# Attention stage with its loop written out, the split of x moved to the start of a period, both halves of a projection together, and four stack slots for the first four tiles

## The reference, cut to what matters

```
x: (8, 512, 256) float32;  H = 16 heads of DH = 16
qkv = (x @ Wqkv).reshape(b, l, 3, H, DH);  q, k, v = qkv[:, :, 0], qkv[:, :, 1], qkv[:, :, 2]
q = q * cos + rotate_half(q) * sin;        k = k * cos + rotate_half(k) * sin
attn = softmax(einsum('bqhd,bkhd->bhqk', q, k) * DH ** -0.5)
out = einsum('bhqk,bkhd->bqhd', attn, v).reshape(b, l, d) @ Wo
x = layernorm(x + out)
x = layernorm(x + ffn(x))     # a shared expert and the best 2 of 8 experts
```

## Time and profile before

| | |
|---|---|
| median of 3 runs (1282.54 to 1285.19) | 1282.6 us |
| the profiled execution, own time | 1286.31 us |
| its span | 1284.4 us |
| granted TensorE clock, mean | 0.969 |
| TensorE / VectorE / ScalarE / GpSimd busy | 1174.9 / 970.9 / 895.0 / 582.5 us |

### The profile page before, as it was taken

The page is one execution under the profiler, slowest core; times in us unless marked ns, Lnnn a source line. Parts: engine busy times, 40 slices in busy tenths (PEclk is TensorE's granted clock), DMA queues, the critical chain, the costliest instruction groups (busy, mean ns, idle before and its releaser), DMA issues. The chain is left out here.

```text
span 1284.4 us, 27380 instructions
## 1 busy us (share of the span) xinstructions
PE 1174.9 (91%) x8369; PEld 864.1 (67%) x8416; DVE 970.9 (76%) x1868; ACT 895.0 (70%) x1970; POOL 582.5 (45%) x591
## 2 busy tenths in 40 slices
PE   3799898989898999879899969999999999999997
PEld 2333333333333333247899969999999999999897
DVE  4788787888787888738766658777777777777596
ACT  3377777777677777647744447777777777777686
POOL 5332222232223220006557745666666666666763
PEclk8699999999999999989899979999999999999999
DMA  6743525252537363532032256777777777776363
GB/s 151 137 82 58 112 53 97 63 110 61 130 96 159 85 155 88 170 125 85 17 112 92 96 170 220 258 237 235 249 251 252 237 238 234 249 252 207 131 187 114
DMA packets 260558, 194.45 MB, mean 151 GB/s; under 512 B 152256, under 2 KB 243392, under 8 KB 260480
## 3 DMA queue, kind: packets, MB, share of 16 engines
q1 hardware_dynamic: 253664, 174.82, 48.2%
q0 software_dynamic: 6816, 18.75, 4.1%
HBM read 122.06 MB, written 37.52 MB: 124 GB/s over the span
## 5 line engine op out<-in xcount | busy, mean ns | idle before, releaser
L464 ACT ACTIVATE att_prob<-att_psB 128x512 f32<-128x512 f32 x512 | 298.3, 608 | 133.1 <-PE att_psB L363 114.0
L553 DVE TENSOR_REDUCE att_mx<-att_psA 128x1 f32<-128x512 f32 x512 | 327.9, 681 | 77.3 <-PE att_psA L353 67.4
L353 PE MATMUL att_psA<-att_qk 96*128 96x512 bf16 x512 | 197.6, 390 | 17.6 <-DVE att_mx L553 6.9
L1650 ACT ACTIVATE exp_psU<-exp_psU,ew_b 128x256 f32<-128x256 f32 x312 | 126.9, 446 | 103.8 <-PE exp_psU L1607 103.8
L363 PE MATMUL att_psB<-att_qk 128*128 128x512 bf16 x465 | 178.4, 387 | 10.2 <-DMA att_qk<-att_mrow 6.1
L1701 DVE CAST exp_hh<-exp_psU 128x512 fp32r<-128x512 f32 x156 | 107.8, 691 | 102.4 <-ACT exp_psU L1650 102.4
L1590 PE MATMUL exp_psD<-exp_w2h,exp_hh 128*128 128x256 f32 x624 | 175.8, 282 | 0.0
L1605 PE MATMUL exp_psU<-exp_xh,exp_w1h 128*128 128x256 f32 x624 | 173.8, 279 | 1.4 <-DVE exp_xl L1692 1.4
L1606 PE MATMUL exp_psU<-exp_xl,exp_w1h 128*128 128x256 f32 x624 | 173.4, 278 | 0.0
L1607 PE MATMUL exp_psU<-exp_xh,exp_w1l 128*128 128x256 f32 x624 | 173.4, 278 | 0.0
L1591 PE MATMUL exp_psD<-exp_w2l,exp_hh 128*128 128x256 f32 x624 | 172.5, 276 | 0.0
(11 more groups left out here) (211 smaller groups left out, 2854.3 us busy)
## 6 DMA issues: line engine op xcount, KB each, us to landing
ew_w<-ew SPq DMA_DIRECT2D x40, 1024.0 KB, 4.9
exp_w<-ew SPq DMA_DIRECT2D x38, 1024.0 KB, 5.8
slots_x<-pre_acc SPq DMA_DIRECT2D x13, 780.0 KB, 4.4
pre_spare<-slots_x SPq DMA_DIRECT2D x39, 260.0 KB, 4.2
out_g<-rows_y SPq DMA_DIRECT2D x32, 256.0 KB, 3.9
ew_b<-eb SPq DMA_DIRECT2D x39, 128.0 KB
pre_spare<-xT SPq DMA_DIRECT2D x8, 512.0 KB, 3.9
attn_rows<-att_ob SPq DMA_DIRECT2D x8, 512.0 KB, 2.8
```

What stands on the lines that cost most here:

```text
L353: pe.matmul(psA[A_BANK[n % U]][:, :], r[:, 0, qt * P:(qt + 1) * P], r[:, 1, :], start=True, stop=True).then_inc(s_amm, 1)
L464: act.activation(prob[:, n % PR, :], psB[B_BANK[n % U]][:, :], ACT.Exp, scale=SCALE).then_inc(s_exp, 1)
L553: dve.reduce_max(mx[:, g % 2, n % U:n % U + 1], psA[A_BANK[n % U]][:, :], AX_X).then_inc(s_max, 1)
```

## The change

- The hardware loop goes: all periods are written out, and semaphore values are constants.
- `x_hi` moves from step 14 to step 0 of its period; `x_lo` moves on GpSimd from the end of that period to its start.
- A projection of queries and keys is issued whole after step 0, product by product instead of half by half.
- Steps: `turn_out` 5 to 6, `norm_out` (5, 6) to (6, 7), `rope` (1, 1, 2) to (1, 2, 2), `copy_max` 9 to 11, `piece_1` 7 to 6, `repeat_1` (8, 9) to (7, 8), `piece_2` 10 to 9, `repeat_2` (11, 12) to (10, 11).
- The first operation of the maxima's split is a scalar_tensor_tensor (m x 0 - m) instead of a tensor_scalar (m x -1).
- The first four tiles have four slots: two in `stack` and two in `prob`, which the first exponential then waits for (`s_tr[1]`). Their first halves are turned as they come, the second halves all after the fourth tile's first. ScalarE makes their pieces, VectorE the last piece of the keys. The set-up on GpSimd starts with the slots' padding.
- w is loaded and split in two parts (queries and keys, then V), with x between them. Four of the first projections have banks of their own.
- SyncE clears the slots from period 1 on, behind the transposes, and loads the attention's rows of a sequence some periods after its store.

```diff
-    ASIDE_QK, ASIDE_V = (1, 3), (0, 1)
...
-    PROJECT_QK, ROPE, COPY_OUT, TURN_OUT, NORM_OUT = (0, 1), (1, 1, 2), 3, 5, (5, 6)
-    PROJECT_V, COPY_V, SPLIT_MAX, TURN_MAX, COPY_MAX = 13, 13, 8, 10, 9
-    PIECE_1, SPREAD_1, PIECE_2, SPREAD_2, SPLIT_X = 7, (8, 9), 10, (11, 12), 14
+    PROJECT_QK, ROPE, COPY_OUT, TURN_OUT, NORM_OUT = 0, (1, 2, 2), 3, 6, (6, 7)
+    PROJECT_V, COPY_V, SPLIT_MAX, TURN_MAX, COPY_MAX = 13, 13, 8, 10, 11
+    PIECE_1, SPREAD_1, PIECE_2, SPREAD_2, SPLIT_X = 6, (7, 8), 9, (10, 11), 0
...
+        ASIDE_QK, ASIDE_V = {1: psA[0], 2: psB[0], 3: psB[1]}, {0: psA[1], 1: psA[2]}
...
-            with eng.Fori(0, passes) as it:
-                for p in range(HEAD, HEAD + BODY):
-                    period(p, it)
...
+            for p in range(-QK_LEAD, NG + 1):
+                period(p)
...
+        def stack_of(tile):
+
+            if tile in (2, 3):
+                some = prob[:, PR // 2 * (tile - 2):PR // 2 * (tile - 1), :].rearrange("p n l -> p (n l)").bitcast(BF16)
+                return some.rearrange("p (i h c) -> p i h c", i=2, h=H)
+            return stack[:, tile % 2]
...
+            CLEAR = [p for p in range(NG) for _ in range((1, 1, 2, 0)[p % NT])][1:CHUNKS + 1]
+            ALL_CLEAR = CLEAR[-1] + 2
+            LOAD = NG - 2 * NT
...
                     turn_heads(tile, 0)
-                    if b < 2 or t >= 2:
+                    if b == 0 and t == NT - 1:
+                        for first in range(NT):
+                            turn_heads(first, 1)
+                    elif b == 1 or b > 1 and t >= 2:
                         turn_heads(tile, 1)
-                    elif t == 1:
+                    elif b > 1 and t == 1:
...
+                for c in range(CHUNKS):
+                    if CLEAR[c] == p:
+                        sp.dma_start(slots[c], blank).then_inc(s_zero, 16)
+                if p == ALL_CLEAR:
+                    sp.wait_ge(s_zero, 16 * CHUNKS)
+                for b in range(B - 1):
+                    if p == max(NT * b + 6, ALL_CLEAR + b):
+                        sp.wait_ge(s_ost[b % 2], 16 * (b // 2 + 1))
+                        norm.load_attention(sp, attn_out, b)
...
+                if t == NT - 1 and valid(b + 1 - 2, B - 2):
+                    x_lo(b + 1)
                 if tile >= FILL:
...
-                if t == NT - 1 and valid(tile + 1 - 2 * NT, NT * (B - 2)):
-                    x_lo(b + 1, it)
...
+                for c in range(DC):
+                    pe.matmul(o, xh[:, b % 2, c, rows], wh[:, c, cols], start=(c == 0), stop=False)
+                if tile == 0:
+                    pe.wait_ge(s_wl, 2 if value else 1)
+                for c in range(DC):
+                    pe.matmul(o, xh[:, b % 2, c, rows], wl[:, c, cols], start=False, stop=False)
+                if t == 0 and not value:
+
+                    pe.wait_ge(s_xl, b + 1)
+                for c in range(DC):
+                    m = pe.matmul(o, xl[:, b % 2, c, rows], wh[:, c, cols], start=False, stop=(c == DC - 1))
...
+                if n == 0:
+                    for k in range(2):
+                        act.wait_ge(s_tr[1][k], 32 * NT // 2)
...
-                    link(dve.tensor_scalar(mstk[:, 0, :], m, -1.0, None, ALU.mult))
+                    link(dve.scalar_tensor_tensor(mstk[:, 0, :], m, 0.0, m, ALU.mult, ALU.subtract))
...
+            def piece_3(tile):
+                st = terms(tile)
+                dve.wait_ge(s_p2, tile + 1)
+                dve.tensor_tensor(st[:, H:, 2, :], heads_of(r1)[:, H:], st[:, H:, 4, :], ALU.subtract).then_inc(s_qsp, 1)
...
+            w_lo(0, slice(0, 2 * D))
+            x_lo(0)
+            w_lo(1, slice(2 * D, 3 * D))
+            x_lo(1)
```

More of the change, by code:

```diff
@@ L166, in attention, with wait, groups @@
         s_dve = a.sem("vector_chain")
[L168 to L181, removed]
-            with eng.Fori(0, passes) as it:
-                for p in range(HEAD, HEAD + BODY):
-                    period(p, it)
[L185 to L188, removed]
+        def wait(eng, s, v):
+            if v > 0:
+                eng.wait_ge(s, v)
+        def groups(period):
+            for p in range(-QK_LEAD, NG + 1):
+                period(p)
         def valid(i, n):
@@ L254, in turn_heads @@
                     sp.dma_start_transpose(qk[:, b % 2, i, some, t * P:(t + 1) * P],
[L255 removed]
+                                           stack_of(tile)[:, i, some, :].rearrange("p h c -> p (h c)")).then_inc(s_tr[half][tile % 2], 16)
             def period(p):
@@ L293, in _ @@
         def _(pool):
[L295 to L311, removed]
-                pool.wait_ge(s_init, k + 1)
@@ L313, in x_lo, with put @@
-            def x_lo(b, it):
-                v = b + 1
-                pool.wait_ge(s_xh, v if it is None else v + it * 2)
+            done = [0]
+            def put(ins):
+                ins.then_inc(s_init, 1)
+                done[0] += 1
+                pool.wait_ge(s_init, done[0])
+            for tile in range(NT):
+                put(pool.memset(stack_of(tile)[:, :, :, KR:], 0.0))
+                put(pool.memset(stack_of(tile)[:, 1, :, KR:KR + PIECES], 1.0))
+            assert done[0] == PADDED
@@ new lines, in _ @@
+            put(pool.memset(zero, 0.0))
+            assert done[0] == BLANK
+            for one in (ident, identf):
+                put(pool.memset(one[:, :], 0.0))
+                put(pool.affine_select(out=one[:, :], in_=one[:, :], compare_op=ALU.not_equal, fill=1.0,
+                                       base=0, pattern=[[-1, P]], channel_multiplier=1))
+            put(pool.memset(V[:, :, :, :, DH + 1:], 0.0))
+            put(pool.memset(V[:, :, :, :, DH:DH + 1], 1.0))
+            put(pool.memset(norm.eps[:, 0:1], 1e-5))
@@ L472, in copy_v, with piece_1 @@
                 b, t = tile // NT, tile % NT
-                wait(act, it, s_vmm, tile + 1, 1)
+                wait(act, s_vmm, tile + 1)
                 if t == 0:
-                    wait(act, it, s_pv, NT * HG * (b - 1), NT)
-                bank = psA[1] if it is None and tile in ASIDE_V else psX
+                    wait(act, s_pv, NT * HG * (b - 1))
+                bank = aside(tile, True) or psX
                 act.activation(V[:, b % 2, t, :, 0:DH], bank[:, 0:D].rearrange("p (h d) -> p h d", d=DH), ACT.Copy).then_inc(s_vev, 1)
-            def piece_1(tile, it):
-                wait(act, it, s_rr, tile + 1, 1)
-                for half in range(2):
-                    wait(act, it, s_tr[half][tile % 2], 32 * (tile // 2), 16)
+            def piece_1(tile):
+                wait(act, s_rr, tile + 1)
+                if tile >= FILL:
+                    for half in range(2):
+                        wait(act, s_tr[half][tile % 2], 32 * (tile // 2))
@@ L514, in period @@
+            w_hi(1, slice(2 * D, 3 * D))
+            x_hi(1)
+            def period(p):
                 for u in range(U):
@@ L596, in norm_out, with rope @@
                                       ALU.mult).then_inc(s_onrm, 1)
-            def rope(tile, k, it):
+            def rope(tile, k):
                 b, t = tile // NT, tile % NT
-                x, half = heads_of(psA[0] if it is None and tile in ASIDE_QK else psX), DH // 2
+                x, half = heads_of(aside(tile, False) or psX), DH // 2
                 def table(tb, c0, c1):
```

309 lines of the change are left out of this document (135 added, 174 removed).

## The result

The changed kernel took 1267.21 us (median of 4 runs, 1265.94 to 1268.2), the kernel before 1283.89 beside it: a ratio of 0.9867, 95% interval 0.9846 to 0.9888. The forecast was 1268.0. The profiled execution took 1267.04 us (span 1265.2), 19.3 less than that of before; on the medians it is 16.7.

The account below looks back on a forecast made before the run. TensorE and VectorE were both nearly full in the attention's steady part, so waits between them matter. Terms -16.1 - 4.4 - 6.2 + 5 + 2.5 + 5 + 0 = -14.2, from 1282.6 to 1268.4 us; range 1250 to 1282.

Parts of the forecast that it names:

- x split at step 0: Six periods with an x split lose their extra 3.78 (twice) or 2.13 us (four times): gain 16.1 us.
- No loop: Both turns of the attention's loop go, 2.21 us each, with the waits' register sums: gain 4.4 us.
- Loads spread: Spreading seven 512 KB attention-row loads removes TensorE's 5.22 us wait for the last maxima copy, plus 1.0: gain 6.2 us.
- The order within a period: VectorE's queue delays the maxima copy by 0.80 us against 0.60 slack; 0.20 in each of 25 periods: loss 5 us.
- (a): In VectorE's queue, the maxima copy moves behind two more row maxima, 0.61 us each: +1.22 us.
- (b): The output's multiplication, formerly in an idle stretch of VectorE, now stands on the path to the maxima copy: +0.33 us.
- (c): The first step of the maxima's split no longer waits for GpSimd's subtraction, on VectorE: -0.78 us.
- The last periods: From the 26th period, without projections, two more maxima before the copy cost about 0.6 us in each of four: loss 2.5.
- Instruction blocks: Straight code fetches throughout, so one maxima copy in every fourth of 25 periods lands 0.8 us late: loss 5 us.
- The fill: Before the first maxima copy, sixteen transposes take 22.04 us of issue whatever their order: 0 us, bounds -4 and +3.
- TensorE decides the period: Rival: VectorE is ahead, TensorE's waits are saved, the period is 14.9 us, another -19, so 1249 us; chance 0.22.
- Fetching is hidden: Rival: instruction blocks come while no maxima copy is under way, so their 5 us loss is 0: 1263 us; chance 0.12.

Follow-up runs that it names:

- straight form: The kernel before with only its hardware loop written out as straight code: 1282.86 us, ratio 0.9965 to the kernel before.
- the old form of the split: The changed kernel with the first operation of the maxima's split back as m x -1 with one input: ratio 0.9844 to the kernel before.
- the fill in turn: The changed kernel with both halves of the first four tiles turned as each tile comes: ratio 0.9841 to the kernel before.

## Why the prediction was right, and where its sizes were off

The forecast came out 0.8 us from the median, and its mechanism is the one that the runs show: the gains of the split, the loop and the loads, less a copy of maxima that became the last to arrive. That it is as near as 0.8 us is luck: the forecast counted from 1282.6, three runs of the kernel before; from the 1283.89 measured beside the changed kernel it would be 2.5 us too high, and in the profiled executions 5.0. Its terms, in its own order:

- *x split at step 0 (gain 16.1).* Right in the periods: none is longer any more. What the term hid is that its two sizes are two causes. TensorE's wait for GpSimd makes 17.40; where the granted clock also falls, the mean to 0.91 between the levels of 2.4 and 1.2 GHz, it is 19.05, another 1.65 (so it is in all twelve such periods of the kernel before and its straight form). The prediction took both sizes as they stood. In the changed order the same late split cost 1.62, not 2.13 to 3.78, so of 16.1 us some 6 belong to the order of before.
- *No loop (gain 4.4).* 4.5 us (2.7 to 6.3), measured alone. The prediction read one turn and took it twice; the second was 2.98, not 2.21.
- *Loads spread (gain 6.2).* The size holds (5 to 8 us with all put back), the step named does not: "seven loads of 512 KB" alone cost 1.1 us of waiting. The constants ahead of them, which the prediction left out, made the rest. The slow scores, for which it added 1.0, come of the granted clock, 0.50 behind the long wait.
- *The order within a period (loss 5).* 0.14 us a period, 3.5 in all; the forecast had 0.20. Points (a), (b) and (c) are borne out: two more maxima and the multiplication stand before the copy, and the split's first step takes 0.16 us. That the subtraction would end "some 0.9 us before the split" came out at 1.04 (350.70 against 351.74). TensorE's own sum, given as 15.2 to 15.3, is nearer to the period: before V's projection TensorE loses 0.56 us (0.59 between starts, less 0.03), not 0.4, and 14.81 + 0.56 = 15.37. So the landing is last, as forecast, but by no more than 0.16 us (the score at 357.54 starts 0.38 after the one before it, where undisturbed ones are 0.22 apart). By this estimate a faster landing alone would bring no more than that; both waits hang on the copy, and no run separates them.
- *The last periods (loss 2.5).* Not measured alone. The loads' 5 us above the changed kernel and their estimated 6.2 leave between a gain of 0.9 and a loss of 0.3 in that stretch, so the term was too high: a period there is 13.80 us (476.28 to 490.08) against 13.59 before (488.06 to 501.65), 0.2 more and not 0.6.
- *Instruction blocks (loss 5).* 5.9 us in all periods beyond 15.41, of which 4.5 are the three with a q8 block and 0.8 is the first, with its lower clock; the kernel before had paid 1.1 for its own late copy at 102.39 (16.35). The forecast spread it as 0.8 us over every fourth period; it came as three of 1.3 to 1.8. That the blocks delay the copy is read from which copies were late: three of three here, and 17 of 17 in the six other kernels with the copy at step 11 or 12. In the three kernels with steps 9 and 10 four of nineteen such copies landed on time, so a block beside the copy is not always enough. No run took the blocks away.
- *The fill (0).* +0.8; its order is worth 1.35 at the first copy and nothing that can be measured at the end.
- *After the attention* 1.8 us fell, which the prediction put at nothing. No run isolates it, and its cause stays open.

Of the rivals, *TensorE decides the period* was right in size about where TensorE's own limit lies ("at best 14.9", measured 14.81 with the copy at step 9) and wrong that the change reaches it: the copy at step 11 keeps it from there. *Fetching is hidden* fell with the three late copies. The Trainium skill's "Runtime: NRT & Kernel Launch", section "Instruction fetch mechanics", holds straight fetching to be hidden by the engine's own pace; that may hold for the engine that fetches, but here a short transfer on its way to TensorE landed late beside a block. The *partly kept split* fell (15.40 us), and so did the *late landing in most periods* (3 of 26).

## What to carry to other kernels

When an instruction of an engine's written-out order feeds a transfer that opens the next period (and, as here, frees the bank that another engine needs next), count what stands before it in that engine's queue: here one more row maximum ahead of the copy cost 0.60 us in every period, and moving the copy two steps back was worth 24 us, more than the 17 of the whole change. Measure the gain of a removed wait in the order where it will be missing, since another wait may already cover part of it. When a small transfer is late, add up all that is still moving when it is issued, not only its nearest neighbours in the queue.

## What the runs showed of the hardware that was not expected

- A period in which a q8 block of 16 KB of instructions went beside the copy of the maxima was 1.33 to 1.82 us longer (16.74 to 17.23 against 15.41), three times of three in the changed kernel; in the first of them the third small transfer landed 3.0 us after its issue, not 1.7.
- The clock decides between the two sizes of a period with a split of x, in all twelve of them in the kernel before and its straight form: 0.91 in the two of the kernel before and the five of its straight form that are 19.05 to 19.12 us long, 1.00 in the other five of 17.38 to 17.51. TensorE's wait does not tell them apart: in the straight form it was 1.99 us at 157.19, where the clock fell, and 2.00 at 222.96, where it did not. Behind the first, two products of the projection start 0.43 us apart (157.76 and 158.19), behind the second 0.23 (223.27 and 223.50).
- VectorE's operation of 0.16 us on 128 x 16 values took 0.96 beside GpSimd's subtraction in either form, with one input in SBUF and with two.
- A late landing can cost more than its own delay: in two other runs of the changed order (the old form of the split, the fill in turn) the copies beside a block at 229.19 and 225.87 came 1.8 to 1.9 us late, the mean granted clock of the period fell to 0.91, and the period was 18.87 and 18.81 us; the one at 275.66 in the changed kernel, 1.8 us late too, kept 1.00 and took 17.23.
